# Which engine rounds the first MLP's output to its high part: ScalarE or VectorE

## The chip, the core and the metric

The kernel runs on one core of one Trainium2 chip. The metric is device time in microseconds (us) of one launch; less is better. The engines that matter here: TensorE (PE) multiplies matrices into PSUM banks; VectorE (DVE), ScalarE (ACT) and GpSimd (POOL) work element by element. Each engine runs its own list of instructions strictly in order, and the lists are tied together by semaphores: an instruction that waits for a semaphore holds up everything behind it on its engine.

## The reference

1024 tokens (32 sequences of 32) of width 256 pass through four layers. Layers 0, 2 and 3 are small adapters: a down projection to 128, gelu, an up projection, an addition and a layer norm, with weights that the sequence's role picks out of three. Layer 1 is attention within each sequence followed by two MLPs, and only its MLP part matters here:

```
attn_out = softmax(q k^T * scale) v @ Wp + bp
cms_out  = gelu(attn_out @ cW1 + cb1) @ cW2 + cb2 + one_hot(target)
modifier = gelu(concat(attn_out, cms_out) @ mW1 + mb1) @ mW2 + mb2
out      = clip(x + cms_out + modifier, 0, 1)
```

cms_out is the first MLP's output. It goes into the second MLP and is also added to the residual.

## The kernel before

Tokens lie along the free axis, features along the partitions. The tokens of layer 1 are worked in two halves of 512, so a tile of 128 features of one half is 128x512, and the 256 features of cms_out are two such tiles, m = 0 and m = 1.

**Split products.** Each matmul operand of layer 1 is held as a high part, rounded to the type float32r, and a low part, which is the value less its high part. A product is three matmuls: high by high, high by low, low by high (`split_matmul`, lines 640 to 642). Each operand must therefore be written twice by an elementwise engine: the rounding copy and the subtraction.

**Phases.** The MLPs run in four phases: phases 0 and 1 are the first MLP on half 0 and half 1, phases 2 and 3 the second MLP on the same halves. A phase has eight steps `hidden(phase, j)`, which give a 128x512 tile of the hidden layer each, and then `outer(phase, ...)`, which multiplies the eight tiles by the second weight. In phases 0 and 1 `hidden` takes 6 matmuls a step, in phase 2 and 3 it takes 12, because cms_out is then a second half of the input. Phase 2 reads the cms_out of phase 0; that of phase 1 is read in phase 3.

**One hidden tile.** PE writes bank 2 + j % 3. ACT computes gelu twice from that bank: once in full (`g_full`, line 1034) and once rounded (`g_h`, line 1037). DVE subtracts the two (`g_l`, line 1412). There are two buffers for `g_full`, so ACT's step n waits until DVE has done step n - 2 (`act.wait_ge(g_ready, n - 1)`). There are three banks in the ring, so PE's step j waits until ACT has done step j - 3.

**The outer step of phases 0 and 1.** For each m, DVE adds the one-hot target and the bias to the bank (`cms_full`, line 1427). Both additions are issued first. ACT rounds each to the high part (`cms_h`, line 1046), and DVE subtracts to get the low part (`cms_l`, line 1433), which waits for ACT's semaphore `cms_high`. At the same time POOL adds `cms_full` to the residual `x1T` (line 1551), once for each m, as soon as that `cms_full` is there.

**What stands around it on each engine.** The function `plan` gives one list of steps, and each engine runs its own part of it in this order. Around the first half it reads `("outer", 0, 0), ("weights", 5), ("hidden", 1, 0), ("hidden", 1, 1), ("weights", 6), ("hidden", 1, 2), ...`, and around the second `("outer", 1, 0), ("weights", 8), ("hidden", 2, 0), ...`. A `weights` step is DVE's alone: it rounds a piece of weights that a DMA has left in `stage` and subtracts (`mw_h` at line 1257, `mw_l` at line 1258, both 128x1024). So behind the outer step DVE has a weights step, then the `g_l` of the first hidden tiles of the next phase, then another weights step.

Of the kernel before, what the change touches and what calls it, by code (L numbers as in the profile page):

```python
# [28 lines left out]
KD = D // P  # L29
# [127 lines left out]
def build(nc, a, out):  # L157

    steps = plan()
    with ExitStack() as ctx:  # L160
        at = [(nc.sbuf_base + 31) // 32 * 32]

        def place(name, shape, dt, offset=None):

            size = 4
            for n in shape[1:]:
                size *= n
            size = (size + 31) // 32 * 32
            if offset is None:
                offset = at[0]  # L170
                at[0] += size
            return nc.alloc_sbuf_tensor_at(name, shape, dt, offset=offset)

        def sem(name):
            return ctx.enter_context(nc.semaphore(name))
# [104 lines left out]
        for name in ("gamma3", "beta3"):  # L280
# [46 lines left out]
        cms = [[place(f"cms0_{x}", [P, KD, HALF], F32R) for x in "hl"],  # L327
               [place(f"cms1_{x}", [P, KD, HALF], F32R, cw2_at + n * 4 * KD * HALF) for n, x in enumerate("hl")]]
        cms_full = place("cms_full", [P, KD, HALF], F32, scratch)
# [99 lines left out]
        outer_ps = sem("outer_ps")  # L429
        cms_full_ready = sem("cms_full_ready")  # L430
        cms_high = sem("cms_high")
# [104 lines left out]
        def _(sp):  # L536
# [18 lines left out]
            def load_roles(columns):  # L555

                _, values = nc.values_load_multi_w_load_instructions(
                    chunk_role_i[0:1, columns.start:columns.stop], engines=[mybir.EngineType.SP], min_val=0, max_val=R - 1,
                    skip_runtime_bounds_check_because="VectorE makes these numbers of two comparisons or clamps them")
                role.update(zip(columns, values))  # L560
# [67 lines left out]
        def _(pe):  # L628
# [97 lines left out]
            def down(layer, c):  # L726

                b = chain_bank(layer, c)
                if layer == 0:
                    take(b, normA_ready, place_of(0, c) + 1)  # L730
                if layer == 3:
                    take(b, normB_ready, c + 1)
                    pe.wait_ge(*zB_done(c))
                    x, done = zB[c % XSLOTS], downB_ps
                else:
                    i = lane_a(layer, c)
                    if layer == 2:
                        take(b, *zB_done(c))
                    pe.wait_ge(xA_ready, i + 1)
                    x, done = xA[i % XSLOTS], downA_ps  # L740
                if c == 0:
                    pe.wait_ge(bu_late_ready if layer else bu_ready, 1)
                pe.wait_ge(hot_ready, 1 if c < MESSY[0] else 2)
                for m in range(KD):
                    pe.matmul(bank[b][:, m * P:(m + 1) * P], x[:, m, :], ident[:, :], start=(m == 0), stop=False,  # L745
                              is_transpose=True, skip_group_check=True)
                pe.matmul(bank[b][:, 0:D], hot[:, c, :], bu[:, (0, 2, 3).index(layer), :], start=False, stop=True,  # L747
                          skip_group_check=True)
                for part, (wd, _, w_in, _, filled) in enumerate(weights_of(layer, c)):
                    pe.wait_ge(w_in, filled)  # L750
                    for k in range(KD):
                        mm = pe.matmul(bank[b][:, D + part * P:D + (part + 1) * P], wd[:, k, :], x[:, k, :],  # L752
                                       start=False, stop=(k == KD - 1), skip_group_check=True)
                mm.then_inc(done, 1)

            def up(layer, c):
                dst = bank[chain_bank(layer, c)][:, 0:D]
                if layer == 3:
                    pe.wait_ge(hB_kept if c in MESSY else hB_ready, like_done(3, c))
                    h, done = hB[c % XSLOTS], upB_ps  # L760
                else:
                    i = lane_a(layer, c)
                    pe.wait_ge(hA_kept if c in MESSY else hA_ready, like_a(layer, c))
                    h, done = hA[i % XSLOTS], upA_ps
                turns = weights_of(layer, c)
                for part, (_, wu, _, w_in, filled) in enumerate(turns):
                    pe.wait_ge(w_in, filled)
                    mm = pe.matmul(dst, h[:, part, :], wu[:, :], start=False, stop=(part == len(turns) - 1),  # L768
                                   skip_group_check=True)
                mm.then_inc(done, 1)  # L770
# [107 lines left out]
        def _(act):  # L878
# [158 lines left out]
                act.activation(g[0][:, j, 0:width], bank[b][:, 0:width], ACT.Gelu,  # L1037
                               bias=bias).then_inc(g_high, 1)

            def outer(phase, part):  # L1040
                if phase < 2:
                    if phase:
                        act.wait_ge(outer_ps, 2 * KD)
                    for m in range(KD):
                        act.wait_ge(cms_full_ready, KD * phase + m + 1)
                        act.copy(cms[phase][0][:, m, :], cms_full[:, m, :]).then_inc(cms_high, 1)

            do = {"vectors": vectors, "chunk_vecs": chunk_vectors, "spread": spread_ids, "seq_vecs": seq_vectors, "fold_transpose": fold_transpose, "fold": fold,
                  "load": load, "down": down, "turn": lambda layer, c: (turn2 if layer else turn0)(c), "values": values, "finish": finish,
                  "project": project, "scores": scores, "mix": mix,  # L1050
                  "hidden": hidden, "outer": outer}
            for name, *args in steps:
                if name in do:
                    do[name](*args)
# [3 lines left out]
        def _(dve):  # L1058
# [359 lines left out]
            def outer(phase, part):  # L1418
                if phase > 2 and part % 4 < 3:
                    return  # L1420
                h = phase % 2
                if phase < 2:
                    if phase:
                        dve.wait_ge(sum_ready, KD)
                    for m in range(KD):
                        dve.wait_ge(outer_ps, KD * phase + m + 1)
                        dve.tensor_tensor(cms_full[:, m, :].rearrange("p (b s) -> p b s", s=S),  # L1427
                                          bank[m][:, :].rearrange("p (b s) -> p b s", s=S),
                                          target[:, m, h * (B // 2):(h + 1) * (B // 2)].unsqueeze(2).to_broadcast([P, B // 2, S]),
                                          ALU.add).then_inc(cms_full_ready, 1)  # L1430
                    for m in range(KD):
                        dve.wait_ge(cms_high, KD * phase + m + 1)
                        dve.tensor_tensor(cms[h][1][:, m, :], cms_full[:, m, :], cms[h][0][:, m, :].bitcast(F32),  # L1433
                                          ALU.subtract).then_inc(cms_ready, 1)
                else:
                    final = phase - 2 + part // 4
                    lo, width = FINALS[final]
                    dve.wait_ge(sum_ready, KD * (lo // HALF + 1))
                    for m in range(KD):
                        dve.wait_ge(outer_ps, KD * (2 + final) + m + 1)  # L1440
                        part = x1T[:, m, lo:lo + width]
                        dve.scalar_tensor_tensor(out=part, in0=bank[2 * (final == 2) + m][:, 0:width],
                                                 scalar=vecs[:, MB2 + m:MB2 + m + 1], in1=part,
                                                 op0=ALU.add, op1=ALU.add).then_inc(x2_ready, 1)
# [132 lines left out]
```

## Time and profile before

| | |
|---|---|
| median of 3 runs | 195.59 us (195.21 to 195.64) |
| the profiled execution's own time | 195.45 us |
| its span, from the first to the last instruction | 193.7 us |
| PE busy | 184.1 us (95%) |
| DVE busy | 114.3 us (59%) |
| ACT busy | 80.8 us (42%) |
| POOL busy | 42.1 us (22%) |
| mean granted TensorE clock | 0.992 |

The span is 1.75 us shorter than the execution's time, and that rest lies outside the instructions. Busy shares are means over stages with different limits; the profile's chain of waits says, for each moment, which engine the end of the run depended on. All times in the rows below are us from the span's start.

### The profile page before, as it was taken

Reading aid. Unit: us, or ns where it says so; the run is one execution under the profiler, and the core shown is the slowest. Engines: PE = TensorE matmul, PEld = TensorE weight load, DVE = VectorE, ACT = ScalarE, POOL = GpSimd, SP = SyncE. Lnnn points to the kernel's source line nnn. Section 1 sums busy time; section 2 is a strip of 40 time slices with the busy share of each in tenths; the row PEclk is TensorE's granted clock in tenths of the full one; section 3 lists DMA queues with packets and bytes.
Section 4 is the critical chain, followed back from the end, with each engine's and each line's share of the span. In section 5 each row is a group of like instructions: output and inputs, shape, how many; then the busy total and the mean of one; then the engine's idle time right before and its main releaser. Section 6 shows DMA issues by size and latency. Waiting matters only on the chain.

```text
span 193.7 us, 3157 instructions
## 1 busy us (share of the span) xinstructions
PE 184.1 (95%) x1031; PEld 157.8 (81%) x1031; DVE 114.3 (59%) x283; ACT 80.8 (42%) x164; POOL 42.1 (22%) x72
## 2 busy tenths in 40 slices
PE   7979999999999999999999999999999999999980
PEld 7858787979888888778888888888888989999860
DVE  2986998799658608982193522041432136558983
ACT  0733764643798206672045544003445333222340
POOL 8474667100000006000140000000100013226431
PEclk9999999999999999999999999999999999999996
DMA  3778589993301130330000060000100003442122
GB/s 103 235 215 277 162 272 270 279 307 125 108 0 46 68 108 0 108 112 0 0 0 3 0 193 24 0 0 5 54 0 0 3 0 108 123 127 69 41 61 77
DMA packets 18874, 17.83 MB, mean 92 GB/s; under 512 B 2145, under 2 KB 17322, under 8 KB 18858
## 3 DMA queue, kind: packets, MB, share of 16 engines
q1 hardware_dynamic: 17008, 14.79, 24.8%
q0 software_dynamic: 928, 2.11, 4.1%
q10 hardware_dynamic: 922, 0.73, 1.2%
q8 instruction: 8, 0.13, 0.3%
q14 instruction: 8, 0.07, 0.1%
HBM read 16.58 MB, written 1.05 MB: 91 GB/s over the span
## 4 chain that ended last, share of the span: by engine, by line
PE 78%; DVE 11%; DMA 5%; issue 2%; ACT 1%; POOL 1%; ACTq 0%; DVEq 0%
PE bank L640 20%; PE bank L641 19%; PE bank L642 19%; PE bank L752 5%; PE bank L768 5%; DMA stage<-in_L_cond_Wq 2%; PE bank L745 2%; DMA x_tok<-in_x,from_row_i 2%; PE bank L821 2%; PE bank L808 2%; PE bank L778 1%; DVE yA L1331 1%; PE bank L747 1%; DVE yB L1350 1%; DVE cms_l L1433 1%
## 5 line engine op out<-in xcount | busy, mean ns | idle before, releaser
L1412 DVE TENSOR_TENSOR g_l<-g_full,g_h 128x512 fp32r<-128x512 f32 x32 | 21.8, 691 | 36.1 <-ACT g_h L1037 36.0
L1034 ACT ACTIVATE g_full<-bank,vecs 128x512 f32<-128x512 f32 x32 | 22.1, 691 | 43.4 <-PE bank L642 40.4
L1524 POOL TENSOR_TENSOR mvA<-mvA,power 128x1 f32<-128x1 f32 x16 | 9.4, 588 | 70.6 <-DVE mvA L1267 70.6
L1037 ACT ACTIVATE g_h<-bank,vecs 128x512 fp32r<-128x512 f32 x32 | 22.0, 687 | 0.0
L1551 POOL TENSOR_TENSOR x1T<-x1T,cms_full 128x512 f32<-128x512 f32 x4 | 6.0, 1498 | 57.2 <-DVE cms_full L1427 57.2
L640 PE MATMUL bank<-g_h,mw_h 128*128 128x256 f32 (+1 forms) x48 | 16.0, 334 | 0.0
L642 PE MATMUL bank<-g_h,mw_l 128*128 128x256 f32 (+1 forms) x48 | 15.3, 318 | 0.0
L641 PE MATMUL bank<-g_l,mw_h 128*128 128x256 f32 (+1 forms) x48 | 15.3, 318 | 0.0
L640 PE MATMUL bank<-ao_h,mw_h 128*128 128x512 f32 x32 | 13.2, 411 | 0.0
L640 PE MATMUL bank<-ao_h,cw_h 128*128 128x512 f32 x32 | 12.8, 400 | 0.1
L642 PE MATMUL bank<-ao_h,mw_l 128*128 128x512 f32 x32 | 12.5, 391 | 0.0
L641 PE MATMUL bank<-ao_l,mw_h 128*128 128x512 f32 x32 | 12.5, 391 | 0.0
L642 PE MATMUL bank<-cms_h,mw_l 128*128 128x512 f32 x32 | 12.5, 390 | 0.0
L642 PE MATMUL bank<-ao_h,cw_l 128*128 128x512 f32 x32 | 12.5, 390 | 0.0
L640 PE MATMUL bank<-cms_h,mw_h 128*128 128x512 f32 x32 | 12.5, 390 | 0.0
L641 PE MATMUL bank<-ao_l,cw_h 128*128 128x512 f32 x32 | 12.5, 390 | 0.0
L640 PE MATMUL bank<-g_h,cw_h 128*128 128x512 f32 x32 | 12.5, 390 | 0.0
L642 PE MATMUL bank<-g_h,cw_l 128*128 128x512 f32 x32 | 12.5, 390 | 0.0
L641 PE MATMUL bank<-cms_l,mw_h 128*128 128x512 f32 x32 | 12.5, 389 | 0.0
L641 PE MATMUL bank<-g_l,cw_h 128*128 128x512 f32 x32 | 12.5, 389 | 0.0
L1331 DVE TENSOR_SCALAR yA<-bank,mvA 128x256 f32<-128x256 f32 x16 | 8.6, 541 | 3.1 <-POOL mvA L1524 3.0
L1427 DVE TENSOR_TENSOR cms_full<-bank,target 128x512 f32<-128x512 f32 x4 | 2.8, 692 | 12.9 <-PE bank L642 12.9
(265 smaller groups left out, 441.5 us busy)
## 6 DMA issues: line engine op xcount, KB each, us to landing
stage<-in_L_cond_mW SPq DMA_DIRECT2D x6, 512.0 KB, 3.3
stage<-in_L_cond_cW SPq DMA_DIRECT2D x4, 512.0 KB, 5.8
wdA<-in_L_cond_W_down SPq DMA_DIRECT2D x14, 128.0 KB, 3.8
wuA<-in_L_cond_W_up SPq DMA_DIRECT2D x14, 128.0 KB, 3.8
wdB<-in_L_cond_W_down SPq DMA_DIRECT2D x12, 128.0 KB, 3.3
wuB<-in_L_cond_W_up SPq DMA_DIRECT2D x12, 128.0 KB, 3.2
wd_last<-in_L_cond_W_down SPq DMA_DIRECT2D x4, 128.0 KB, 2.3
wu_last<-in_L_cond_W_up SPq DMA_DIRECT2D x4, 128.0 KB, 2.3
```

Of the source, the lines that this page charges most:

```text
L640: pe.matmul(dst, w[0], x[0], start=first, stop=False)
L641: pe.matmul(dst, w[0], x[1], start=False, stop=False)
L642: return pe.matmul(dst, w[1], x[0], start=False, stop=last)
L745: pe.matmul(bank[b][:, m * P:(m + 1) * P], x[:, m, :], ident[:, :], start=(m == 0), stop=False, is_transpose=True, skip_group_check=True)
L752: mm = pe.matmul(bank[b][:, D + part * P:D + (part + 1) * P], wd[:, k, :], x[:, k, :], start=False, stop=(k == KD - 1), skip_group_check=True)
L768: mm = pe.matmul(dst, h[:, part, :], wu[:, :], start=False, stop=(part == len(turns) - 1), skip_group_check=True)
L1034: act.activation(g_full[n % 2][:, 0:width], bank[b][:, 0:width], ACT.Gelu, bias=bias)
L1037: act.activation(g[0][:, j, 0:width], bank[b][:, 0:width], ACT.Gelu, bias=bias).then_inc(g_high, 1)
L1331: dve.tensor_scalar(yA[k][:, :], bank[chain_bank(layer, c)][:, 0:D], mvA[:, k, 0:1], mvA[:, k, 2:3], ALU.subtract, ALU.mult).then_inc(norm ...
L1412: dve.tensor_tensor(g[1][:, j, 0:width], g_full[n % 2][:, 0:width], g[0][:, j, 0:width].bitcast(F32), ALU.subtract).then_inc(g_ready, 1)
L1524: pool.tensor_tensor(mv[:, k, 2:3], mv[:, k, 1:2], power[:, :], ALU.pow).then_inc(done, 1)
L1551: pool.tensor_tensor(half, half, cms_full[:, m, :], ALU.add).then_inc(sum_ready, 1)
```

## The change

ACT no longer takes part in the outer step of phases 0 and 1. DVE does the rounding copy itself, for each m directly ahead of the subtraction. DVE's order in the step becomes: both additions, then copy, subtract for m = 0, then copy, subtract for m = 1. The wait of ACT for `outer_ps` in phase 1 (the high part lies where the weights `cw2` were) goes with it; DVE's additions wait for the same semaphore. Nothing else moves.

```
             def outer(phase, part):          # ScalarE
-                if phase < 2:
-                    if phase:
-                        act.wait_ge(outer_ps, 2 * KD)
-                    for m in range(KD):
-                        act.wait_ge(cms_full_ready, KD * phase + m + 1)
-                        act.copy(cms[phase][0][:, m, :], cms_full[:, m, :]).then_inc(cms_high, 1)
...
             def outer(phase, part):          # VectorE
                     for m in range(KD):
+                        dve.wait_ge(cms_full_ready, KD * phase + m + 1)
+                        dve.tensor_copy(cms[h][0][:, m, :], cms_full[:, m, :]).then_inc(cms_high, 1)
                         dve.wait_ge(cms_high, KD * phase + m + 1)
                         dve.tensor_tensor(cms[h][1][:, m, :], cms_full[:, m, :], cms[h][0][:, m, :].bitcast(F32),
                                           ALU.subtract).then_inc(cms_ready, 1)
```

## Rows read from the trace of the kernel before

**Rows 1.** The page: busy share of each engine; granted clock in 40 slices.
```profile
PE 184.1 (95%) x1031; PEld 157.8 (81%) x1031; DVE 114.3 (59%) x283; ACT 80.8 (42%) x164; POOL 42.1 (22%) x72
...
PEclk9999999999999999999999999999999999999996
```

**Rows 2.** Chain of waits, 73.9 to 84.5 us: start, length on chain, what.
```profile
75.41 1.62 DVE cms_l L1433
```

**Rows 3.** Timeline of DVE, 74 to 84 us: start, duration, line, operation, out<-in.
```profile
74.03 0.69 DVE L1427 TENSOR_TENSOR cms_full<-bank,target 128x512 f32<-128x512 f32 x1 [0.67 <-PE bank L642]
74.64 0.68 DVE L1433 TENSOR_TENSOR cms_l<-cms_full,cms_h 128x512 fp32r<-128x512 f32 x1
...
76.95 0.68 DVE L1257 CAST mw_h<-stage 128x1024 fp32r<-128x1024 f32 x1
77.67 1.22 DVE L1258 TENSOR_TENSOR mw_l<-stage,mw_h 128x1024 fp32r<-128x1024 f32 x1
78.81 1.29 DVE L1412 TENSOR_TENSOR g_l<-g_full,g_h 128x512 fp32r<-128x512 f32 x2
80.01 0.69 DVE L1257 CAST mw_h<-stage 128x1024 fp32r<-128x1024 f32 x1
...
81.88 1.29 DVE L1412 TENSOR_TENSOR g_l<-g_full,g_h 128x512 fp32r<-128x512 f32 x2
```

**Rows 4.** Timeline of ACT, 79 to 83 us; brackets: idle before, releaser.
```profile
79.59 0.69 ACT L1034 ACTIVATE g_full<-bank,vecs 128x512 f32<-128x512 f32 x1 [1.57 <-DVE g_l L1412]
...
82.66 0.69 ACT L1034 ACTIVATE g_full<-bank,vecs 128x512 f32<-128x512 f32 x1 [0.65 <-PE bank L642]
```

**Rows 5.** Timeline of POOL, 72 to 77 us.
```profile
73.44 1.29 POOL L1551 TENSOR_TENSOR x1T<-x1T,cms_full 128x512 f32<-128x512 f32 x1 [37.58 <-DVE cms_full L1427]
...
74.80 1.68 POOL L1551 TENSOR_TENSOR x1T<-x1T,cms_full 128x512 f32<-128x512 f32 x1
```

**Rows 6.** Timeline of PE, 80 to 84 us.
```profile
80.41 0.39 PE L642 MATMUL bank<-ao_h,cw_l 128*128 128x512 f32 x1
80.91 0.50 PE L640 MATMUL bank<-ao_h,cw_h 128*128 128x512 f32 x1
...
83.33 0.39 PE L641 MATMUL bank<-ao_l,cw_h 128*128 128x512 f32 x1
83.56 0.39 PE L642 MATMUL bank<-ao_h,cw_l 128*128 128x512 f32 x1
83.98 0.50 PE L640 MATMUL bank<-ao_h,cw_h 128*128 128x512 f32 x1
```

**Rows 7.** Groups by line and shape: count, busy us, mean ns, idle before.
```profile
L1372 DVE CAST x1b_h<-x1T 128x512 fp32r<-128x512 f32 x2 | 0.8, 404 | 0.0
...
L1046 ACT CAST cms_h<-cms_full 128x512 fp32r<-128x512 f32 x4 | 2.5, 622 | 17.8 <-DVE cms_full L1427 9.6 <-PE bank L642 8.1
```

**Rows 8.** Timeline of DVE and of POOL, 21 to 23.5 us.
```profile
21.81 0.72 DVE L1240 CAST bu_high<-bu_rows 128x512 fp32r<-128x512 f32 x1
...
21.71 0.54 POOL L1509 MEMSET probs_T<- 128x512 f32 x1
```

**Rows 9.** Timeline of DVE, 97 to 103 us.
```profile
97.22 0.69 DVE L1433 TENSOR_TENSOR cms_l<-cms_full,cms_h 128x512 fp32r<-128x512 f32 x1
...
97.95 1.68 DVE L1433 TENSOR_TENSOR cms_l<-cms_full,cms_h 128x512 fp32r<-128x512 f32 x1
99.55 0.68 DVE L1257 CAST mw_h<-stage 128x1024 fp32r<-128x1024 f32 x1
...
101.41 0.69 DVE L1412 TENSOR_TENSOR g_l<-g_full,g_h 128x512 fp32r<-128x512 f32 x1
```

**Rows 10.** Timeline of POOL, 98 to 99 us.
```profile
97.34 1.73 POOL L1551 TENSOR_TENSOR x1T<-x1T,cms_full 128x512 f32<-128x512 f32 x1
```

**Rows 11.** Timeline of ACT, 104 to 105 us.
```profile
104.73 0.69 ACT L1034 ACTIVATE g_full<-bank,vecs 128x512 f32<-128x512 f32 x1 [1.45 <-PE bank L642]
```

**Rows 12.** Timeline of PE, 12 to 13 us.
```profile
12.57 0.41 PE L723 MATMUL bank<-ident,x_tok 128*128 128x128 f32 x2 [0.83 <-DMA x_tok<-in_x,from_row_i]
```

More of the change, by code:

```diff
@@ L1038, in hidden @@
                                bias=bias).then_inc(g_high, 1)
-            def outer(phase, part):
-                if phase < 2:
-                    if phase:
-                        act.wait_ge(outer_ps, 2 * KD)
-                    for m in range(KD):
-                        act.wait_ge(cms_full_ready, KD * phase + m + 1)
-                        act.copy(cms[phase][0][:, m, :], cms_full[:, m, :]).then_inc(cms_high, 1)
             do = {"vectors": vectors, "chunk_vecs": chunk_vectors, "spread": spread_ids, "seq_vecs": seq_vectors, "fold_transpose": fold_transpose, "fold": fold,
@@ L1050, in _ @@
                   "project": project, "scores": scores, "mix": mix,
-                  "hidden": hidden, "outer": outer}
+                  "hidden": hidden}
             for name, *args in steps:
```

## The prediction

> **What bounds the kernel now.** I read the page first: PE is busy for 95% of the span, DVE for 59%, ACT for 42%, and the clock stands at its upper level (2.4 GHz) until the last slice [rows 1]. So what a change off PE is worth depends on whether PE ever waits for it. Next I read the chain of waits. Between 73.8 and 80.9 us it leaves PE: it goes through the step that is changed, with 1.62 us in one `cms_l`, then through DVE's weights step and `g_l`, then ACT, and comes back to PE at 80.91 [rows 2, 6]. From there it stays on PE until 181.6 us. Last, I read the timelines of the engines around both outer steps.
>
> In the first half's stage DVE is what is late. It runs with no gap above 0.1 us from 74.03 to past 83: additions, two `cms_l`, a weights step, two `g_l`, a second weights step, two more `g_l` [rows 2, 3]. ACT's step hidden(1, 2) starts at 79.59 after an idle 1.57 us, 0.09 behind the end of the first of the two `g_l` that start at 78.81 (78.81 + 0.69 = 79.50) [rows 3, 4]. PE's step hidden(1, 5) needs ACT's hidden(1, 2) for its bank, and it starts at 80.91 where its beat (starts 0.23 us apart, 83.33 and 83.56) would have put it at 80.64: 0.27 us lost [rows 6]. The same happens once more: the `g_l` at 81.88 ends at 82.57, ACT's hidden(1, 4) starts at 82.66 (the row names PE, but this is 0.09 behind `g_l` again), and PE's hidden(1, 7) starts at 83.98 [rows 3, 4, 6]. Both late starts of PE hang on one unbroken run of DVE. A delay of DVE ahead of 78.81 reaches 80.91 and 83.98 in the same size, and counts once.
>
> **Why DVE is late there.** A 128x512 subtraction takes 0.68 to 0.69 us, but the second `cms_l` takes 1.62 [rows 2, 3]. POOL's second addition runs from 74.80 to 76.48 beside it, and takes 1.68 where the first took 1.29 [rows 5]. They exclude each other: the addition, 1.29 long, really ran from 75.19 (76.48 - 1.29), 0.13 before the first `cms_l` ended at 75.32, and the second `cms_l` ended 0.55 behind the addition's end (77.03 - 76.48). The second half shows the same: the addition ends at 99.07, `cms_l` at 99.63, 0.56 behind [rows 9, 10].
>
> **The change part by part.** *Removed:* four ACT copies of 0.62 us [rows 7], two in each half, and the wait of each `cms_l` for them. Whatever ACT gains by it in the first half is worth nothing, because ACT finishes hidden(1, 1) and then idles 1.57 us for DVE [rows 4]. I cost this at 0; with that cover gone it would be worth at most the 0.62 of one copy.
>
> *Added:* four DVE copies of 128x512. The same form took 0.40 us (two at line 1372) [rows 7]. One took 0.72: it stood beside a POOL memset that ended at 22.25, and ended 0.28 behind it (22.53) [rows 8]. So such a copy also waits for POOL. The low part now waits for a copy of DVE's own; `mw_h` and `mw_l` show that step: 76.95 + 0.68 = 77.63, and `mw_l` starts at 77.67, so 0.04 of gap, where unlinked instructions overlap by about 0.08 (76.95 against 77.03) [rows 3].
>
> *The first half, step by step.* The additions are unchanged and the first new copy starts where `cms_l` started, at 74.64. POOL's first addition ends at 74.73 (73.44 + 1.29) [rows 5], which a `cms_l` started at 74.64 did not feel (0.68); even if the copy does, 74.73 + 0.28 = 75.01 is no later than its own end.
> - Copy 0: 74.64 + 0.40 = 75.04.
> - POOL's second addition, asking since 74.80, gets through 0.13 before that, at 74.91, and ends at 76.20.
> - Subtraction 0 could start at 75.08 and is stopped by the addition: it ends 0.55 behind it, at 76.75.
> - Copy 1 starts 0.08 before that and takes 0.40: 76.67 to 77.07.
> - Subtraction 1: 77.11 to 77.80.
> - `mw_h` starts 0.08 before that, at 77.72, against 76.95: **0.77 us later**.
>
> Everything behind it on DVE moves by that much: weights 5, `g_l` of hidden(1, 0) and (1, 1), weights 6, `g_l` of (1, 2). PE's idle time before 80.91 grows from 0.27 to 1.04 us, and 83.98 becomes 84.75. After that PE runs on its own beat to 181.6, so the shift stays. Weights 5 also releases a DMA of a piece that is needed 20 us later; its delay costs nothing.
>
> *Bounds.* At the low end the addition gets through at once, at 74.80, ends at 76.09, and the rest follows as above: 0.11 less, 0.66. At the high end POOL's second addition goes ahead of the first copy: addition to 76.09, copy 0 to 76.37 (+ 0.28), subtraction 0 to 77.10, copy 1 from 77.02 to 77.42, subtraction 1 from 77.46 to 78.15, `mw_h` at 78.07: 1.12. A further end, below nothing, is a rival below. I take 0.77, since the copy asks 0.16 before the second addition.
>
> *The second half.* The same sum gives: copy 0 from 97.22 to 97.62, addition to 98.78 (97.62 - 0.13 + 1.29), subtraction 0 to 99.33, copy 1 to 99.65, subtraction 1 to 100.38, `mw_h` at 100.30 against 99.55: 0.75 late. The `g_l` at 101.41 would end at 102.85 instead of 102.10. ACT's hidden(2, 2), which needs it, starts at 104.73, released by PE [rows 9, 11]. So 2.6 us of cover, of which 0.75 is used; phase 2 also reads the cms_out of the first half, not of this one. Cost 0; without the cover it would be 0.75.
>
> **Sum.** 195.45 (the profiled execution: span 193.7 and 1.75 outside it) + 0.77 = 196.22. The runs' median, 195.59, is 0.14 above this execution, which would make it 196.36. I say 196.3 us, 0.4% slower.
>
> **Rivals.**
> *A, DVE keeps POOL out (not slower).* If the subtraction follows each copy so closely that POOL's second addition doesn't get in, DVE runs four instructions in a row: copy 74.64 to 75.04, subtraction 75.08 to 75.77, copy 75.69 to 76.09, subtraction 76.13 to 76.82, `mw_h` at 76.74: 0.21 earlier than now, time 195.24 by the execution, 195.4 by the median. The point from which it decides is the 0.04 us gap at 75.04. For it: POOL's result isn't needed for 20 us, so nothing would punish it. Against it: with the same gap of 0.04 (97.91 to 97.95) POOL got in ahead of the waiting `cms_l` in the second half [rows 9, 10]. The Trainium skill ("Perfetto Trace Analysis", section "Optimizing Scalar/DVE Operations") says that an operation that either engine can do is faster on VectorE where its 2x or 4x mode is available, and that moving it to ScalarE makes sense where VectorE is saturated. The trace bears out the first clause for the single copy (0.40 against 0.62) and the second for this stage; by the first clause alone the time would be A's. A has 0.14.
>
> *B, POOL first (slower still).* The upper bound above, 1.12 us: 196.6 to 196.7. For it: the copy stood back behind a memset at 21.81. Against: it asks earlier here. 0.12.
>
> *C, part of the shift is caught later.* If PE's second late start, 83.98, hung on something that doesn't move (the weights' DMA, say), its loss would shrink: 83.98 stands 0.19 behind the beat (0.42 since the start before it, less 0.23), so 0.77 - 0.19 = 0.58, some 196.0 to 196.2. Against: the weights step at 80.01 starts right behind `g_l`, waiting for no DMA [rows 3], and the 0.42 us from 83.56 to 83.98 ends just behind the gelus of ACT's hidden(1, 4), which `g_l` released [rows 4, 6]. 0.06.
>
> *D, the clock.* PE's idle 1.04 us would be the longest since its first matmul; the longest now is 0.83 us, up to 12.57, and the clock stayed at its upper level around it [rows 1, 12]. Were it to fall for a while, the time would be well above B's. 0.03.
>
> **How the numbers follow.** The forecast itself has 0.65, from 196.0 to 196.5 (0.66 to 0.77, from 195.45 or 195.59, and the spread of the runs). Two tenths of a per cent, 0.39 us, is about what a measurement of this kernel can tell from no change. Forecast, B and D are slower by more, and most of C: 0.83. I take 0.79, since a misread lock order can fall between A and the forecast. Within 0.2%: A and such middles, 0.17. Faster: 0.04. The range reaches down to the middles between A and the forecast and up past B: 195.6 to 196.9.
>
> **What would show it.** In the changed kernel: four DVE copies at about 0.40; the first subtraction of each half stretched to about 1.6 us, the second at 0.69; POOL's second addition shorter (about 1.4); `mw_h` 0.8 us later behind the additions than now (2.92 us behind the start at 74.03); ACT's idle before hidden(1, 2) some 2.3 us instead of 1.57; PE idle some 1 us before hidden(1, 5), and the same distances after it; hidden(2, 2) of ACT still released by PE. The prediction is wrong if PE's idle time there doesn't grow, or if both subtractions run at 0.69.

## The result, and the profile after

The changed kernel takes 196.44 us (median of 20 runs, 195.82 to 198.72), the kernel before 195.58 (20 runs beside it): ratio 1.0047, 95% interval 1.0028 to 1.0067, so about 0.9 us slower. Its profiled execution took 196.43 us, its span is 194.6.

The page of the changed kernel, busy shares and granted clock, against [rows 1]: DVE does 1.5 us more, ACT 2.4 us less, the clock is as it was.

```profile
PE 184.4 (95%) x1031; PEld 158.1 (81%) x1031; DVE 115.8 (60%) x287; ACT 78.4 (40%) x160; POOL 41.6 (21%) x72
...
PEclk9999999999999999999999999999999999999996
```

The timeline of DVE in the changed kernel behind the first outer step (start, duration, line, operation), against [rows 3]; lines behind 1046 have moved up by eight, so 1425 is the new copy, 1427 the subtraction, 1249 `mw_h`, and `g_l`, in rows further down, 1404.

```profile
74.25 0.69 DVE L1419 TENSOR_TENSOR cms_full<-bank,target 128x512 f32<-128x512 f32 x1 [0.67 <-PE bank L642]
74.85 0.42 DVE L1425 CAST cms_h<-cms_full 128x512 fp32r<-128x512 f32 x1
75.30 1.67 DVE L1427 TENSOR_TENSOR cms_l<-cms_full,cms_h 128x512 fp32r<-128x512 f32 x1
76.89 0.41 DVE L1425 CAST cms_h<-cms_full 128x512 fp32r<-128x512 f32 x1
77.34 0.69 DVE L1427 TENSOR_TENSOR cms_l<-cms_full,cms_h 128x512 fp32r<-128x512 f32 x1
77.95 0.69 DVE L1249 CAST mw_h<-stage 128x1024 fp32r<-128x1024 f32 x1
```

POOL's second addition beside it, against [rows 5]:

```profile
75.02 1.41 POOL L1545 TENSOR_TENSOR x1T<-x1T,cms_full 128x512 f32<-128x512 f32 x1
```

The stretched subtraction has changed places. It is now the first, 1.67 us, because POOL's addition got in behind the first copy and ended at 76.43; the subtraction ended 0.54 behind it, at 76.97. The second runs in its plain 0.69. `mw_h` starts 3.70 us behind the start of the second addition (77.95 - 74.25); before it was 2.92.

What ACT and PE then do in the changed kernel, against [rows 4, 6]:

```profile
80.59 0.69 ACT L1034 ACTIVATE g_full<-bank,vecs 128x512 f32<-128x512 f32 x1 [2.36 <-DVE g_l L1404]
```

```profile
80.62 0.39 PE L642 MATMUL bank<-ao_h,cw_l 128*128 128x512 f32 x1
81.91 0.50 PE L640 MATMUL bank<-ao_h,cw_h 128*128 128x512 f32 x1 [0.91 <-ACT g_h L1037]
...
84.54 0.39 PE L642 MATMUL bank<-ao_h,cw_l 128*128 128x512 f32 x1
84.98 0.50 PE L640 MATMUL bank<-ao_h,cw_h 128*128 128x512 f32 x1
```

ACT idles 2.36 us for `g_l` instead of 1.57. PE's start of hidden(1, 5) lies 1.29 us behind the start before it instead of 0.50, and that of hidden(1, 7) 0.44 instead of 0.42. The shift happens once, at 81.91.

The second half, against [rows 9, 11]: one row of DVE in the kernel before, the start of its second addition, then DVE and ACT in the changed kernel.

```profile
96.57 0.69 DVE L1427 TENSOR_TENSOR cms_full<-bank,target 128x512 f32<-128x512 f32 x1 [0.60 <-PE bank L642]
```

```profile
97.56 0.69 DVE L1419 TENSOR_TENSOR cms_full<-bank,target 128x512 f32<-128x512 f32 x1 [0.60 <-PE bank L642]
98.16 0.45 DVE L1425 CAST cms_h<-cms_full 128x512 fp32r<-128x512 f32 x1
98.65 1.66 DVE L1427 TENSOR_TENSOR cms_l<-cms_full,cms_h 128x512 fp32r<-128x512 f32 x1
...
101.29 0.69 DVE L1249 CAST mw_h<-stage 128x1024 fp32r<-128x1024 f32 x1
...
103.15 0.68 DVE L1404 TENSOR_TENSOR g_l<-g_full,g_h 128x512 fp32r<-128x512 f32 x1
```

```profile
105.72 0.69 ACT L1034 ACTIVATE g_full<-bank,vecs 128x512 f32<-128x512 f32 x1 [1.45 <-PE bank L642]
```

DVE is late here too: `mw_h` starts 3.73 us behind the second addition, where it was 2.98 (99.55 less 96.57). But `g_l` ends at 103.83 and ACT's hidden(2, 2) waits for PE until 105.72, with the same idle 1.45 us as before. Nothing of it reaches PE.

**A measure that doesn't drift.** The profiled executions differ by up to 1 us in when the first MLP begins on PE (49.87 to 50.84 us over the twelve profiled here), for reasons ahead of this stage. So the experiments are read from one difference inside each trace: from the start of DVE's first addition of phase 0 to the first matmul of phase 2 on PE, called the stage below. In the kernel before it is 23.70 us (72.67 to 96.37), in the changed kernel 24.48 (72.88 to 97.36): +0.78. The two ends of the stage, before and after:

```profile
72.67 0.69 DVE L1427 TENSOR_TENSOR cms_full<-bank,target 128x512 f32<-128x512 f32 x1 [5.56 <-PE bank L642]
96.37 0.39 PE L640 MATMUL bank<-ao_h,mw_h 128*128 128x512 f32 x1
```

```profile
72.88 0.69 DVE L1419 TENSOR_TENSOR cms_full<-bank,target 128x512 f32<-128x512 f32 x1 [5.56 <-PE bank L642]
97.36 0.39 PE L640 MATMUL bank<-ao_h,mw_h 128*128 128x512 f32 x1
```

Behind the stage the traces agree: from that first matmul of phase 2 to the start of DVE's last instruction on the chain it is 94.07 to 94.09 us in all twelve. The stage of the kernel before, profiled twice, came to 23.70 and 23.67 us.

### The profile page after: what moved, and what is told of

Its sections match the earlier page's. It is cut to its first block, busy times and chain, and to the rows that moved or that the text cites. A ratio compares the mean times of both kernels' runs of the same rounds, so it can differ in the third digit from the quotient of the medians.

```text
span 194.6 us, 3156 instructions
## 1 busy us (share of the span) xinstructions
PE 184.4 (95%) x1031; PEld 158.1 (81%) x1031; DVE 115.8 (60%) x287; ACT 78.4 (40%) x160; POOL 41.6 (21%) x72
## 4 chain that ended last, share of the span: by engine, by line
PE 76%; DVE 13%; DMA 4%; issue 2%; ACT 1%; POOL 1%; ACTq 0%; DVEq 0%
PE bank L640 19%; PE bank L642 19%; PE bank L641 19%; PE bank L752 5%; PE bank L768 5%; DMA stage<-in_L_cond_Wq 2%; PE bank L745 2%; DMA x_tok<-in_x,from_row_i 2%; PE bank L821 2%; PE bank L808 2%; PE bank L778 1%; DVE mw_l L1250 1%; DVE yA L1323 1%; DVE cms_l L1427 1%; PE bank L747 1%
## 5 line engine op out<-in xcount | busy, mean ns | idle before, releaser
L1545 POOL TENSOR_TENSOR x1T<-x1T,cms_full 128x512 f32<-128x512 f32 x4 | 5.4, 1356 | 58.3 <-DVE cms_full L1419 58.2
```

The lines of the kernel that those rows point to most:

```text
L1545: pool.tensor_tensor(half, half, cms_full[:, m, :], ALU.add).then_inc(sum_ready, 1)
```

## The experiments

The theory (T): the cost lies in the first half alone, where DVE's unbroken run holds PE up one to one; and its size comes from DVE's copies and subtractions and POOL's additions keeping each other out. Rivals: every moved copy costs its share (R1), the difference isn't in this stage (R2), POOL has no part (R3), ACT's rounding is worth something by itself (R4), the second half's ACT copies cost something (R5). Except for the control, every kernel differs from the kernel before or from the changed one only as its diff shows. The stage is read from one profiled execution of each kernel; the ratio compares some 12 runs (20 for the changed kernel, 7 for the kernel before with late additions) with the kernel before, measured beside them.

| kernel | stage, us | against before | ratio of times, interval |
|---|---|---|---|
| changed | 24.48 | +0.78 | 1.0047 (1.0028 to 1.0067) |
| first half only | 24.49 | +0.79 | 1.0041 (1.0021 to 1.0061) |
| second half only, three times | 23.68, 23.68, 23.71 | -0.02 to +0.01 | 0.9976 (0.9959 to 0.9992), 0.9977 (0.9936 to 1.0018), 0.9982 (0.9949 to 1.0016) |
| before itself, as control | 23.67 | -0.03 | 0.9986 (0.9951 to 1.0021) |
| before, late additions | 22.92 | -0.78 | 0.9931 (0.9899 to 0.9962) |
| changed, late additions | 23.52 | -0.18 | 0.9985 (0.9965 to 1.0004) |
| changed, in order, late additions | 22.99 | -0.71 | 0.9950 (0.9919 to 0.9981) |
| changed, in order, early additions | 24.93 | +1.23 | 1.0042 (1.0007 to 1.0077) |
| changed, one copy more | 24.98 | +1.28 | 1.0068 (1.0034 to 1.0101) |

### Only the first half, only the second half

```
-                if phase < 2:                   # ScalarE, outer
+                if phase == 1:                  # first half only (phase == 0: second half only)
...
+                        if phase == 0:          # VectorE, outer (phase == 1: second half only)
+                            dve.wait_ge(cms_full_ready, KD * phase + m + 1)
+                            dve.tensor_copy(cms[h][0][:, m, :], cms_full[:, m, :]).then_inc(cms_high, 1)
```

> Only the first half's two copies (phase 0) go to VectorE; the second half's stay on ScalarE. Theory T (VectorE's unbroken run behind the first outer step holds PE up, and nothing else of the change counts): the whole cost, +0.77 us against the kernel before, mw_h 3.70 us behind the start of the second addition (2.92 before), PE's start of hidden(1, 5) about 1.29 us behind the start of its last matmul before it (0.50 before). Rival R1 (every copy moved costs its share, in both halves): +0.4 us. Rival R2 (the difference is not in this stage but in how the program as a whole lies and starts): any value near 0, unrelated to PE's idle time.

> Only the second half's two copies (phase 1) go to VectorE. Theory T: no change in the time (within 0.1 us), although mw_h of weights 8 starts 0.75 us later behind the second addition (3.73 instead of 2.98), because hidden(2, 2) has some 2.6 us of cover. Rival R1: +0.4 us. Rival R2: any value, as in the first-half run.

The first half alone has the whole cost: +0.79 us in the stage, 196.57 us. PE's timeline of that kernel shows the same 1.29 us between two starts as the changed kernel:

```profile
81.01 0.39 PE L642 MATMUL bank<-ao_h,cw_l 128*128 128x512 f32 x1
82.30 0.50 PE L640 MATMUL bank<-ao_h,cw_h 128*128 128x512 f32 x1 [0.91 <-ACT g_h L1037]
```

The second half alone leaves the stage as it was, although its DVE timeline has the copies and the late `mw_h`, 3.73 us behind the second addition:

```profile
97.09 0.69 DVE L1427 TENSOR_TENSOR cms_full<-bank,target 128x512 f32<-128x512 f32 x1 [0.60 <-PE bank L642]
...
100.82 0.68 DVE L1257 CAST mw_h<-stage 128x1024 fp32r<-128x1024 f32 x1
```

Its time came out 0.24% under the kernel before, with an interval that leaves out 1. The trace had no place for a gain, so it was run again, and a third time beside the kernel before as a control.

> The second half's copies alone on VectorE, once more, since its first runs were 0.24% under the kernel before with no difference in the trace from 50 us on. Theory T: 0 within 0.1 us. Rival R5 (ScalarE's copies of the second half did cost something, such as 0.4 us): 0.2% faster again, and some wait in the second half's stage that is shorter.

> The second half's copies alone on VectorE, third time, beside the kernel before as a control. Theory T: no further from 1.000 than the control by more than 0.1%. Rival R5: again 0.2% faster.

> The kernel before itself, unchanged, as one of the compared kernels: what this measurement calls a difference where there is none. Theory T: ratio 1.000, with an interval that shows whether the 0.23% of the second-half runs can be told from nothing. Rival R5 (those runs were really faster): this one lies within 0.1%, and the second-half run beside it again 0.2% under.

The control, which differs from the kernel before in nothing, came to 0.9986, the third run beside it to 0.9982, both with intervals of 0.3 to 0.4% to either side. All three runs stand some 0.2% under, and the control's interval takes in that as well as nothing, so the times alone don't settle R5. The traces speak against it: the stage with the second half moved is 23.68 to 23.71 us, in the two traces of the kernel before 23.67 and 23.70, and behind the stage all of them take 94.08 or 94.09. A gain of 0.2%, 0.4 us, would have to lie ahead of the stage, where the moved copies haven't run yet. R1 falls with the split of the two halves; R2 falls because the stage holds the difference, and nothing behind it does.

### POOL's additions moved away

```
                 if phase < 2:                   # GpSimd, outer
+                    pool.wait_ge(g_ready, JT * (phase + 2))
                     for m in range(KD):
                         pool.wait_ge(cms_full_ready, KD * phase + m + 1)
```

The additions now start at 88.7 and 120.0 us (89.1 and 120.3 in the changed kernel), while DVE waits.

> The kernel before (copies on ScalarE), but GpSimd's additions to the residual wait for the low parts of the next phase's eight hidden tiles (g_ready 16 and 24), where VectorE is idle. Theory T with the shared port (a GpSimd addition and VectorE's copies and subtractions exclude each other): the second cms_l falls from 1.62 to 0.69 us, mw_h starts 1.99 us behind the second addition instead of 2.92, both late starts of PE in hidden(1, 5) and (1, 7) go (0.27 + 0.19 us, and about 0.11 of slow restart each), so 0.5 to 0.75 us faster than before, about 195.0. Rival R3 (the long cms_l is ScalarE's or the memory's doing and GpSimd has no part in it): no change, cms_l stays at 1.6 us.

> The changed kernel (copies on VectorE) with the same late GpSimd additions. Theory T with the shared port: VectorE runs copy, subtraction, copy, subtraction without a stop (0.42, 0.69, 0.41, 0.69), mw_h 2.71 us behind the second addition, so 0.21 earlier than in the kernel before: 0.2 us faster than before, 1.0 us faster than the changed kernel. Rival R3 (GpSimd has no part in it): as the changed kernel, +0.8 us, with a subtraction of 1.67 us still there.

The timeline of DVE with ACT's copies and late additions (the kernel before otherwise):

```profile
74.41 0.69 DVE L1427 TENSOR_TENSOR cms_full<-bank,target 128x512 f32<-128x512 f32 x1 [0.67 <-PE bank L642]
75.02 1.46 DVE L1433 TENSOR_TENSOR cms_l<-cms_full,cms_h 128x512 fp32r<-128x512 f32 x2
76.40 0.69 DVE L1257 CAST mw_h<-stage 128x1024 fp32r<-128x1024 f32 x1
```

Two subtractions take 1.46 us together instead of 2.39, and `mw_h` comes 1.99 us behind the second addition, as expected. PE no longer waits: between 79.4 and 84 us its starts lie 0.22 to 0.23 us apart throughout. The stage is 0.78 us shorter, and the time 194.57 us (195.66 for the kernel before beside it). Both are a little more than was expected, 0.5 to 0.75 us and about 195.0. In the kernel before, the two late starts and the one right behind each lie 0.50, 0.34, 0.42 and 0.33 us behind the start ahead, where the beat is 0.23: 0.67 us. The rest lies in starts of 0.23 to 0.24 us behind them, where this kernel has 0.22 to 0.23.

The same with DVE's copies:

```profile
74.06 0.69 DVE L1419 TENSOR_TENSOR cms_full<-bank,target 128x512 f32<-128x512 f32 x1 [0.67 <-PE bank L642]
74.67 0.42 DVE L1425 CAST cms_h<-cms_full 128x512 fp32r<-128x512 f32 x1
75.12 0.69 DVE L1427 TENSOR_TENSOR cms_l<-cms_full,cms_h 128x512 fp32r<-128x512 f32 x1
75.73 0.42 DVE L1425 CAST cms_h<-cms_full 128x512 fp32r<-128x512 f32 x1
76.19 0.69 DVE L1427 TENSOR_TENSOR cms_l<-cms_full,cms_h 128x512 fp32r<-128x512 f32 x1
76.80 0.69 DVE L1249 CAST mw_h<-stage 128x1024 fp32r<-128x1024 f32 x1
```

All four instructions run at their plain length; `mw_h` is at 2.74 behind the second addition, 0.18 ahead of the kernel before, and the stage is shorter by the same 0.18. The ratio of times, 0.9985, doesn't tell this kernel from the kernel before. R3 falls in both kernels. And with POOL out of the way the copies, in this order, still cost 0.60 us of stage (23.52 less 22.92): POOL is not the whole reason.

### Each tile whole: the order of DVE, with and without POOL

```
                     for m in range(KD):         # VectorE, outer; phase < 2
                         dve.wait_ge(outer_ps, KD * phase + m + 1)
...
                                           ALU.add).then_inc(cms_full_ready, 1)
-                    for m in range(KD):
                         dve.wait_ge(cms_full_ready, KD * phase + m + 1)
                         dve.tensor_copy(cms[h][0][:, m, :], cms_full[:, m, :]).then_inc(cms_high, 1)
```

The first of the two kernels has the late additions as well, the second has POOL's additions where they were.

> All four copies on VectorE and the late GpSimd additions, but VectorE takes each tile whole: addition, copy, subtraction for m = 0, then for m = 1, so that the copy and subtraction of m = 0 use the 0.67 us in which VectorE waits for the second bank. Theory T (what counts is when VectorE reaches mw_h and g_l, not which engine rounds): mw_h 3.36 us behind the start of the first addition (kernel before 4.28, with late additions alone 3.35), no late start of PE in hidden(1, 5) and (1, 7), and the time of the run with late additions and ScalarE's copies, 0.5 to 0.75 us under the kernel before. Rival R4 (ScalarE's rounding is worth something in itself, as work taken off VectorE): slower than that run by about the two copies, 0.8 us, so no faster than before.

> VectorE takes each tile whole (addition, copy, subtraction for m = 0, then for m = 1), and GpSimd's additions stay where they are in the kernel before. Theory T with the shared port: now each subtraction meets a GpSimd addition (the first at 0.77 us behind the first addition of VectorE, the second behind the second), both subtractions take 1.67 us, the second addition of VectorE is pushed back too, and mw_h starts 5.57 us behind the start of the first addition (kernel before 4.28, changed kernel 5.07): 1.3 us slower than the kernel before, slower than the changed kernel, although the same order with late GpSimd additions gained 0.8 us in the trace. Rival R3 (the order of VectorE's own instructions decides, GpSimd doesn't matter): as fast as that run.

DVE of the first kernel, with late additions:

```profile
72.39 0.69 DVE L1419 TENSOR_TENSOR cms_full<-bank,target 128x512 f32<-128x512 f32 x1 [5.56 <-PE bank L642]
73.12 0.43 DVE L1424 CAST cms_h<-cms_full 128x512 fp32r<-128x512 f32 x1
73.58 0.69 DVE L1426 TENSOR_TENSOR cms_l<-cms_full,cms_h 128x512 fp32r<-128x512 f32 x1
74.19 0.69 DVE L1419 TENSOR_TENSOR cms_full<-bank,target 128x512 f32<-128x512 f32 x1
...
75.98 0.69 DVE L1249 CAST mw_h<-stage 128x1024 fp32r<-128x1024 f32 x1
```

The stage is 0.71 us shorter than before and nearly that of ACT's copies (0.78): DVE can round for itself at almost no cost, if it does so in the 0.67 us in which it waits for the second bank anyway. R4 falls: the time is 0.50% under the kernel before, where R4 had it no faster, and the intervals don't tell it from the run with ACT's copies (0.9931). The expectation for `mw_h` was short by 0.23 us (3.59 behind the first addition instead of 3.36): each copy now follows its own addition and starts 0.72 to 0.73 us behind it, where an instruction that needn't wait for the one ahead starts 0.61 behind; I had not counted that link.

With early additions the same order costs most of all but the kernel with one copy more, below. DVE and POOL of that kernel:

```profile
72.68 0.69 DVE L1419 TENSOR_TENSOR cms_full<-bank,target 128x512 f32<-128x512 f32 x1 [5.56 <-PE bank L642]
73.40 0.43 DVE L1424 CAST cms_h<-cms_full 128x512 fp32r<-128x512 f32 x1
73.86 1.67 DVE L1426 TENSOR_TENSOR cms_l<-cms_full,cms_h 128x512 fp32r<-128x512 f32 x1
75.46 0.68 DVE L1419 TENSOR_TENSOR cms_full<-bank,target 128x512 f32<-128x512 f32 x1
76.17 0.43 DVE L1424 CAST cms_h<-cms_full 128x512 fp32r<-128x512 f32 x1
76.63 1.66 DVE L1426 TENSOR_TENSOR cms_l<-cms_full,cms_h 128x512 fp32r<-128x512 f32 x1
78.21 0.68 DVE L1249 CAST mw_h<-stage 128x1024 fp32r<-128x1024 f32 x1
```

```profile
73.45 1.53 POOL L1544 TENSOR_TENSOR x1T<-x1T,cms_full 128x512 f32<-128x512 f32 x1 [37.58 <-DVE cms_full L1419]
76.21 1.53 POOL L1544 TENSOR_TENSOR x1T<-x1T,cms_full 128x512 f32<-128x512 f32 x1 [1.23 <-DVE cms_full L1419]
```

Each copy starts 0.04 to 0.05 us ahead of a POOL addition and holds it up (1.53 instead of 1.29), the addition gets through behind the copy, and both subtractions are stretched. DVE's order is that of the kernel with late additions, and only POOL's part differs: the stage is 1.94 us longer for it (24.93 against 22.99). `mw_h` lies 5.53 us behind the first addition (5.57 expected), the stage is 1.23 us longer than before. The times (196.79 us, +0.42% with a wide interval) show it slower than before, but can't tell it from the changed kernel; the traces can, by 0.45 us.

### One copy more

```
                         dve.wait_ge(cms_full_ready, KD * phase + m + 1)
+                        if (phase, m) == (0, KD - 1):
+                            link(dve.tensor_copy(cms[h][0][:, m, :], cms_full[:, m, :]))
                         dve.tensor_copy(cms[h][0][:, m, :], cms_full[:, m, :]).then_inc(cms_high, 1)
```

> The changed kernel with one rounding copy more in the first half: that of m = 1 is done twice, one behind the other. Theory T (VectorE's lateness reaches PE one to one): mw_h 0.45 us later than in the changed kernel (4.15 behind the second addition), PE's idle time before hidden(1, 5) 0.45 longer (start to start 1.74 instead of 1.29), time 0.45 us above the changed kernel, about 1.2 to 1.3 above the kernel before. Rival R2 (the difference isn't in this stage): no change against the changed kernel.

PE's timeline of that kernel:

```profile
80.03 0.39 PE L642 MATMUL bank<-ao_h,cw_l 128*128 128x512 f32 x1
81.79 0.50 PE L640 MATMUL bank<-ao_h,cw_h 128*128 128x512 f32 x1 [1.37 <-ACT g_h L1037]
```

1.76 us between the starts, 0.47 more than in the changed kernel for one copy and its link (0.45 expected), and 0.50 more in the stage. `mw_h` lies 4.17 us behind the second addition, also 0.47 later. So PE paid for this added DVE work in full. The ratios of times, 1.0068 and 1.0047, have intervals that overlap; it is the traces that show it.

## Why the prediction was right

It gave 196.3 us within 195.6 to 196.9, slower; 196.44 was measured. By its own steps:

- *The place.* One run of DVE behind the first outer step, with two late starts of PE that hang on it and count once. Shown by the half that has the whole cost, by the unchanged distance of the second late start (0.42, now 0.44), and by the added copy.
- *The sum.* In it, 0.77 us were worked out for `mw_h`; it came 0.78 later (3.70 less 2.92), and PE's wait grew by 0.79. The single terms held: copies 0.42 and 0.41 (0.40 taken), first subtraction stretched and the second not, POOL's addition 1.41 (1.40 expected: 76.20 less 74.80). That the whole time came within 0.2 us of 196.3 says less: the runs of one kernel spread by more than that.
- *The exclusion between DVE and POOL*, which the trace of before had shown on two stretched subtractions and one copy, and from which the order copy, addition, subtraction followed. Shown by the late additions and, for the order, by the early ones with each tile whole. The Trainium skill ("SBUF — State Buffer", section "Who interferes with whom") puts it so: "Issue order, not op shape, decides who blocks". The traces agree: which of the two subtractions takes 1.6 us has changed from the second to the first to both, with the same shapes.
- *The second half at nothing.* Shown: 0.75 us late on DVE, nothing on PE.
- *Rival A*, DVE keeping POOL out, was wrong about who gets in: the addition got through in the gap behind the copy, both times. Its price was right: with POOL away the stage was 0.18 us shorter (0.21 worked out). *B* and *C* didn't happen: the copy went ahead of the addition, and nothing was caught later (from the first matmul of phase 2 to DVE's last instruction on the chain 94.09 us before, 94.08 after). *D* didn't happen: the mean clock was 0.992 before and 0.991 after, and the row of 40 slices is the same.
- The rule that such an operation is faster on VectorE where a faster mode is to be had (the Trainium skill, "Perfetto Trace Analysis", section "Optimizing Scalar/DVE Operations") holds here for the instruction (0.42 against 0.62 us) and not for the kernel, whose stage it made 0.8 us longer, since DVE was the late engine there, though busy for only 59% of the span. The rule's other half, on a saturated VectorE, is the one that applies if it is read for this stage alone.

What is not explained: the time moved by 0.86 us (medians), the stage by 0.78, and the kernel with late additions gained 1.1 us by the medians, 1.35 by the ratio, for 0.78 in the stage. The intervals cover these differences. In the profiled executions nothing is left over: before and after differ by 0.98 us (196.43 less 195.45), of which 0.78 lie in the stage, 0.21 ahead of it (it starts at 72.88 instead of 72.67), and none behind. Why the start of the stage moves from execution to execution stays open.

## What to carry to other kernels

An engine that is busy 59% of the span can be the late one in the stage that matters: follow the chain from PE's late start back, and where one engine runs without a gap up to that start, price an added instruction on it one to one, whatever the shares say. Before moving work between engines look for what already stands in that run for no need: here POOL's addition, for which nothing waits until DVE needs the buffer of `cms_full` again at 95.28, some 19 us later, cost DVE 0.93 us. Letting it wait took 0.78 us off the stage with ACT's copies and 0.96 with DVE's; the choice of the rounding engine is worth 0.78 with early additions, 0.60 with late ones, and next to nothing (0.07) with late ones once DVE takes each tile whole. Where two halves of a loop get the same edit, ask for each what comes next: here the second half had 2.6 us of cover and the first none.

## What the runs showed of the hardware

The start of the first MLP on PE varied between 49.87 and 50.84 us over the profiled executions, and by 0.68 us (50.11 to 50.79) for one and the same kernel, that of the second half alone, which is nearly the size of the effect looked for; the control's ratio, 0.9986, has an interval of 0.7% in width.

Not every DVE instruction keeps POOL out: in the kernel before, the second addition of `cms_full`, which reads one input from a PSUM bank, took its plain 0.69 us beside POOL's first addition, which took its plain 1.29 [rows 3, 5]. The copies and the subtractions, whose inputs all lie in SBUF, do: both were held up by POOL or held it up in the rows above.

The exclusion changes hands faster than the profiled ends suggest: a subtraction of two SBUF tiles ends 0.54 to 0.56 us behind the end of a POOL addition that held it up, though it takes 0.69 by itself, and POOL's addition, if its own part takes 1.29 us, starts that part some 0.13 before the profiled end of the DVE instruction ahead of it (75.14, which is 76.43 less 1.29, against 75.27 in the changed kernel).
